# Attention over 8,704 keys: TensorE issues one step at a time (scores, maxima, values) where the scores of two steps stood together

## What is computed

```
k = jnp.concatenate([k_x, k_l], axis=2)          # 8192 context keys + 512 latent keys
v = jnp.concatenate([v_x, v_l], axis=2)
sim = jnp.einsum('bhid,bhjd->bhij', q, k)        # 512 queries x 8704 keys
attn = jax.nn.softmax(sim, axis=-1)
out = jnp.einsum('bhij,bhjd->bhid', attn, v)
```

## Time and profile before

| what | value |
|---|---|
| three runs | 2238.9, 2241.94, 2242.02 us; median 2241.94 |
| profiled execution | 2242.18 us, span 2240.4 us |
| TensorE busy over the span | 2144.8 us (96%) |
| VectorE, ScalarE, GpSimd busy | 1612.3, 1103.8, 902.5 us |
| attention phase in the trace | about 481 to 1064 us |
| loads of keys and values (res and vb), median from issue to landing | 3.3, 5.4 and 5.6 us |

### The profile page before, as it was taken

How to read it: one execution, slowest core, us unless ns; L and a number is a source line. 1 busy time by engine, 2 the same in 40 slices (tenths; PEclk the granted TensorE clock), 3 DMA queues, 4 the chain that set the end, 5 groups by cost and what they waited for, 6 DMA issues and landing times. The chain is left out here.

```text
span 2240.4 us, 37583 instructions
## 1 busy us (share of the span) xinstructions
PE 2144.8 (96%) x12843; PEld 1082.3 (48%) x12843; DVE 1612.3 (72%) x2356; ACT 1103.8 (49%) x1726; POOL 902.5 (40%) x634
## 2 busy tenths in 40 slices
PE   5899999999999999999899999999999999999976
PEld 2344444433333333333475665757566575756533
DVE  6687777659989999887575757667585666657563
ACT  4122332334444444555464655656474565647445
POOL 0235555559989999600221303122130212213044
PEclk9999999999999999999999999999999999999989
DMA  3345454433322322432323333342333334233313
GB/s 116 130 162 168 167 201 163 148 117 90 93 85 86 97 84 85 124 105 71 125 95 110 98 122 85 132 123 89 114 93 130 85 132 123 81 118 95 116 40 112
DMA packets 159854, 252.75 MB, mean 113 GB/s; under 512 B 11506, under 2 KB 63986, under 8 KB 159730
## 3 DMA queue, kind: packets, MB, share of 16 engines
q1 hardware_dynamic: 159730, 250.96, 35.4%
HBM read 211.73 MB, written 36.70 MB: 111 GB/s over the span
## 5 line engine op out<-in xcount | busy, mean ns | idle before, releaser
L67 PE MATMUL scores<-xt_hi,wt_hi 128*128 128x256 f16 (+3 forms) x1568 | 413.2, 275 | 10.2 <-DVE xt_lo L1418 4.6
L68 PE MATMUL scores<-xt_lo,wt_hi 128*128 128x256 bf16 (+3 forms) x1568 | 413.5, 275 | 0.0
L69 PE MATMUL scores<-xt_hi,wt_lo 128*128 128x256 f16 (+3 forms) x1568 | 413.0, 275 | 0.0
L1375 POOL TENSOR_TENSOR l_rstd<-l_var_eps,neg_half 128x1 f32<-128x1 f32 x71 | 66.6, 938 | 834.6 <-DVE l_var_eps L1429 834.6
L900 DVE TENSOR_REDUCE pmax<-mx 128x1024 f32 (+1 forms) x196 | 239.9, 1224 | 34.5 <-PE mx L1085 22.3
L69 PE MATMUL l_tok<-wt_hi,h_lo 128*128 128x512 f16 x576 | 219.5, 381 | 0.0
L1658 ACT ACTIVATE wt_hi<-stage 128x512 f16<-128x512 f32 x384 | 213.6, 615 | 8.6 <-DMA stage<-in_L_attn_Wf 8.6
L1098 PE MATMUL scores<-q_hi,res 128*128 128x512 f16 x544 | 209.0, 384 | 2.7 <-ACT q_lo L997 1.3
L1099 PE MATMUL scores<-q_lo,res 65*128 65x512 f16 x544 | 207.9, 382 | 0.0
L67 PE MATMUL l_tok<-wt_hi,h_hi 128*128 128x512 f16 x512 | 195.6, 382 | 0.0
L68 PE MATMUL l_tok<-wt_lo,h_hi 128*128 128x512 bf16 x512 | 195.4, 382 | 0.0
(11 more groups left out here) (321 smaller groups left out, 4745.8 us busy)
## 6 DMA issues: line engine op xcount, KB each, us to landing
stage<-in_L_attn_Wf SPq DMA_DIRECT2D x60, 1024.0 KB, 5.2
keys<-wt_hi SPq DMA_DIRECT2D x136, 128.0 KB
res<-keys SPq DMA_DIRECT2D x68, 256.0 KB, 3.3
vb<-values SPq DMA_DIRECT2D x68, 256.0 KB, 5.6
stage<-in_ctx SPq DMA_DIRECT2D x16, 1024.0 KB, 10.0
values<-wt_lo SPq DMA_DIRECT2D x16, 1024.0 KB
stage<-in_L_ffn_f SPq DMA_DIRECT2D x16, 1024.0 KB, 5.3
res<-keys SPq DMA_DIRECT2D x68, 128.0 KB, 5.4
```

The costliest lines, as they stand in the source:

```text
L67: pe.matmul(out, lh, rh, start=first, stop=False, **kw)
L68: pe.matmul(out, lh, rl, start=False, stop=False, **kw)
L69: return pe.matmul(out, ll, rh, start=False, stop=last, **kw)
L1375: g.tensor_tensor(rstd[:, t:t + 1], var_eps[:, t:t + 1], k.neg_half[:, 0:1], ALU.pow).then_inc(rstd_done, 1)
```

## The change

The loop over pairs of steps becomes a loop over single steps. For step j TensorE now issues S(j+2), M(j), W(j), where it issued S(j+2), S(j+3), M(j), W(j), W(j+1), M(j+1) for two. The instructions, their number and their waits are otherwise the same; no other engine's order and no transfer is changed.

```diff
                 def block_steps(p, b, i=0):
                     last = isinstance(i, int) and b == KB - 1
-                    for j in range(0, SUB, 2):
-                        for n in range(2):
-                            if j + 2 < SUB:
-                                scores(p, b, i, j + 2 + n)
-                            elif not last:
-                                scores(p, b + 1, i, n)
-                            elif p + 1 < PAIRS:
-                                if n == 0:
-                                    pe.wait_ge(rows_done, 2 * (p + 2))
-                                scores(p + 1, 0, 0, n)
+                    for j in range(SUB):
+                        if j + 2 < SUB:
+                            scores(p, b, i, j + 2)
+                        elif not last:
+                            scores(p, b + 1, i, j + 2 - SUB)
+                        elif p + 1 < PAIRS:
+                            if j == 2:
+                                pe.wait_ge(rows_done, 2 * (p + 2))
+                            scores(p + 1, 0, 0, j + 2 - SUB)
                         if isinstance(i, int) and b == 0 and j == 0:
                             if p:
                                 pe.wait_ge(pv_copied, p)
                             t_.matmul(pv[:], zero[:], k.q_hi[:, 0, :], start=True, stop=False)
                         tile_max(p, b, i, j)
-                        for n in range(2):
-                            weigh(p, b, i, j + n, last and j + n == SUB - 1)
-                        tile_max(p, b, i, j + 1)
+                        weigh(p, b, i, j, last and j == SUB - 1)
```

## The result

The changed kernel is slower: 2276.66 us median (2276.45 to 2276.77, 4 runs) against 2241.98, a ratio of 1.0165 [1.0151, 1.0178]. Measured again, beside more runs of before, the ratio was 1.0173 [1.0159, 1.0187]. That is 35 to 39 us; the prediction had 49.

What follows compares the result with a forecast made beforehand. TensorE was taken to bound the kernel before, at 2.18 us a step in pairs 0 to 2. 43 us there plus 8.5 in pair 3 less 3 for pair starts gave 48.5 more: 2291 us, range 2272 to 2303.

Steps and rivals of the forecast that it cites:

- the two causes: TensorE's extra switches between matmul kinds, 33 us in all, and a chain of waits through four engines, 2.40 us a step.
- The price of a switch: On TensorE, 0.09 us on leaving S, 0.05 on entering W, 0.10 on leaving W; 24.5 and 8.5 us, 33 in all.
- W alone between two other kinds: On TensorE, a single W between other matmul kinds: bounds 0.91 and 1.01 us, 1.01 taken.
- The estimate of 14 us for this term: TensorE's switches priced by the skill's drain of some 128 cycles: 0.05 us more a step instead of 0.12, 14 us instead of 33.
- The chain closes: M through W, S, exponential, GpSimd's addition, VectorE's row sum and maximum to M three steps on: 7.20 us, 2.40 a step; 65%.
- To the next R 0.10: Link on VectorE from the end of the row sum to the start of the next maximum R, put at 0.10 us.
- The signs: In pairs 0 to 2: exponentials 2.40 us apart, GpSimd 0.3 idle before additions, M right behind R about once in three steps.
- The last eight steps of pair 2: Steps without an M: no added cost, as TensorE's 2.0 us a step is under GpSimd's 2.16.
- A worse lock: Rival, 8%: GpSimd's addition waits up to 0.27 us for a row sum begun in a pause; 2.49 a step, 2312 us.
- Pair 3: Last pair, only S and W on TensorE: 1.98 us a step against 1.855, 8.5 us more over 68 steps.
- The rival of the switches alone: Rival, 18%: row sums find GpSimd's pauses, no chain of waits forms, only TensorE's 33 us of switches count: 2275 us.
- The wait doesn't wear off: M's wait for the maximum in pairs 0 to 2 persists, since a shift of TensorE delays the exponential and GpSimd too.

Runs made afterwards that it cites:

- With 960 columns: Changed kernel with GpSimd adding 960 columns instead of 896 in pairs 0 to 2, VectorE 64: 2272.32 us, ratio to before 1.0146.

## Why the prediction was right, and too high

The sign, the two causes and the range (2272 to 2303) held; the point, 2291, was 14 us too high.

- TensorE bounds both stages before the change: right. Without the row sum the phase hardly changes (0.4 us).
- The price of a switch, from the earlier trace rows: right. 33 us were forecast for the switches alone, and the two kernels without row sums are 33 us apart. W alone between two other kinds takes 1.01, the upper of the two bounds. The estimate of 14 us for this term, worked out from the drain in the Trainium skill ("TensorE: Matmul & The Clock Gate", "Step-by-step: what each phase is for"), falls: a step of pair 3 got 0.13 longer, not 0.05.
- The chain closes: right, link by link, and over three steps. Its length is the term that was mis-sized: 7.20 us were forecast, 7.02 measured. "To the next R 0.10" was the failing link; it makes up the 0.18 of difference. In the earlier trace rows R starts 0.10 after the row sum's end, but it also starts 0.54 after M; it was M that it waited for. Where the row sum is what holds it, R starts 0.08 before the row sum's record ends (557.19 and 556.01 + 1.26). The maximum also takes 1.21 then, not 1.23; other links are 0.01 longer. So the step is 2.34, not 2.40, and pairs 0 to 2 lost 32.2 us, where 43 less 3 were forecast. The signs came in the same measure: exponentials 2.34 and not 2.40 apart, GpSimd idle 0.24 and not 0.3 between two additions, and M right behind R in 142 of 195 steps and not in one of three.
- The last eight steps of pair 2, which have no M, were put at nothing, as GpSimd's 2.16 would hide TensorE's 2.0. They took 17.03 us from S to S before and 17.95 after, with exponentials 1.99 apart: GpSimd held nothing there, and the term was 0.9 us.
- A worse lock, in which GpSimd's addition waits for a row sum, did not come: the additions last 2.08 as before.
- Pair 3: 8.5 us forecast, 7.9 measured.
- Phase: 48.5 forecast, 40.15 measured, 8.3 of the 14. The other 6 are not in the working at all: the profiled execution on which the sum was made had 6 us more in the rest of the program than that of after.
- The rival of the switches alone gave 2275, nearer to 2276.7 than the forecast. It is not what happened: M waits in most steps. It has the number by luck, because the row sum's 7 us and the 6 of the rest cancel.
- "The wait doesn't wear off": right for this kernel. With 960 columns it wasn't there in two pairs of three, so it is no law of this loop.

## What to carry to other kernels

On TensorE group matmuls of one kind as far as the buffers allow, and count the borders: here each round of S and W costs 0.24 us, whether it holds one step, two or three. A change that looks local moves every wait that hangs on the order: follow one chain through all engines, around to where it began, and divide by the steps it spans. For each link ask whether its two ends really wait for each other in the row from which it is taken, or whether a third signal came at the same time. And compare the stage, not the whole, when the rest varies by more than the error that you look for.

## What the hardware showed beside that

A row sum on VectorE that waits for GpSimd's addition ends a fixed time after it, by its own size: 0.08 us for 64 columns, 0.15 for 128, 0.28 for 256. For 64 and 128 columns this holds also where GpSimd has only 0.08 us between two additions. The Trainium skill ("SBUF — State Buffer", "Who interferes with whom") says that the second to issue is blocked for the whole instruction. The traces bear it out for a VectorE row sum behind a GpSimd addition, mostly 0.93 to 1.35 us long there, for 128 columns, and 0.27 where it didn't wait. What it means for a loop of both engines, two ways to run that each lasted for whole pairs and differ by 0.06 us a step (with 960 columns), was not expected.
